# Row maxima of the attention scores: one reduction over two PSUM banks for two query tiles, in place of one reduction per tile

## What is computed

```python
x = x + xattn(ctx, layernorm(x), mask)      # 8 heads of 32, 512 queries x 512 keys per batch and head
scores = einsum('bthd,bshd->bhts', q, k) / sqrt(32)
scores = where(src_mask == 0, -inf, scores)
attn = softmax(scores, axis=-1)             # the row maximum is subtracted before exp
x = x + ffn(layernorm(x))                   # 16 experts, top 8, and one shared expert
```

## Time and profile before

| what | value |
|---|---|
| median of 3 runs | 1065.43 us (1065.13 to 1066.44) |
| profiled execution: span from the first to the last instruction | 1056.2 us |
| median less that span | 9.2 us |
| mean granted TensorE clock | 0.992 |
| busy share of the span | PE 96%, PEld 73%, DVE 61%, ACT 44%, POOL 37% |
| max matmuls | 256, the first at 27.6 us, the last at 426.5 us |
| reductions to maxima | 256, 683 ns median, 173.3 us together |

### The profile page before, as it was taken

How to read it: one execution, slowest core, us unless ns; L and a number is a source line. 1 busy time by engine, 2 the same in 40 slices (tenths; PEclk the granted TensorE clock), 3 DMA queues, 4 the chain that set the end, 5 groups by cost and what they waited for, 6 DMA issues and landing times.

```text
span 1056.2 us, 14941 instructions
## 1 busy us (share of the span) xinstructions
PE 1012.5 (96%) x5198; PEld 773.3 (73%) x5198; DVE 647.5 (61%) x1469; ACT 465.9 (44%) x865; POOL 389.0 (37%) x355
## 2 busy tenths in 40 slices
PE   4789999999999998899999999999999999999998
PEld 3656767676767665567888888888888888888886
DVE  5877777877777557355565555555555555555544
ACT  3346565656665646545323323333333333332322
POOL 3379797879797967345210010010010100100000
PEclk9899999999999999999999999999999999999999
DMA  7343433434333223324222121121220230221220
GB/s 239 104 131 78 131 81 111 108 84 131 73 110 75 65 65 105 92 86 131 75 80 61 52 80 50 61 81 40 72 80 31 71 90 20 91 80 31 93 68 20
DMA packets 65674, 87.87 MB, mean 83 GB/s; under 512 B 10720, under 2 KB 31088, under 8 KB 65600
## 3 DMA queue, kind: packets, MB, share of 16 engines
q1 hardware_dynamic: 63680, 84.83, 28.0%
q10 hardware_dynamic: 1920, 2.10, 0.6%
HBM read 56.97 MB, written 4.46 MB: 58 GB/s over the span
## 4 chain that ended last, share of the span: by engine, by line
PE 91%; DVE 4%; ACT 2%; SPq 1%; issue 1%; DMA 1%; POOL 0%; DVEq 0%; ACTq 0%
PE ps L653 50%; PE pst L653 18%; PE ps L732 6%; PE ps L759 5%; PE pst L748 5%; PE ps L659 4%; PE ps L772 1%; DVE mx L1201 1%; ACT e_buf L868 1%; SPq L606 1%; PE ps L811 1%; SPq L541 1%; ACT ctx_h L868 0%; DVE wsrc_l L1148 0%; PE ps L812 0%
## 5 line engine op out<-in xcount | busy, mean ns | idle before, releaser
L653 PE MATMUL ps<-x_h,weights 128*128 128x512 f32 x1088 | 365.6, 397 | 1.4 <-DVE x L1194 0.8
L653 PEld LDWEIGHTS ps<-x_h,weights 128*128 128x128 f32 x1088 | 204.5, 188 | 51.8 <-issue 1.0
L1201 DVE TENSOR_REDUCE mx<-ps 128x1 f32<-128x512 f32 x256 | 173.3, 685 | 81.8 <-PE ps L732 80.9
L868 ACT ACTIVATE hh<-qb 128x512 fp32r<-128x512 f32 x136 | 86.0, 632 | 296.4 <-DVE qb L1315 273.7
L653 PE MATMUL ps<-x_l,weights 128*128 128x512 f32 x544 | 214.6, 395 | 0.0
L653 PE MATMUL pst<-hh,weights 128*128 128x512 f32 x544 | 194.6, 399 | 0.0
L1304 DVE TENSOR_TENSOR qb<-ps,sg 128x512 f32<-128x512 f32 x136 | 94.1, 692 | 160.2 <-PE ps L653 153.8
L868 ACT ACTIVATE e_buf<-pst 128x512 f32<-128x512 f32 x256 | 147.4, 596 | 92.8 <-PE pst L748 81.8
L1317 DVE TENSOR_TENSOR hl<-qb,hh 128x512 fp32r<-128x512 f32 x136 | 94.3, 693 | 95.0 <-ACT hh L868 95.0
L1407 POOL TENSOR_TENSOR e_sums<-e_sums,e_buf 128x1024 f32<-128x1024 f32 x60 | 143.5, 2391 | 7.2 <-ACT e_buf L868 1.2
L1359 POOL TENSOR_SCALAR ve<-mv 128x4 f32<-128x4 f32 x8 | 1.8, 226 | 347.1 <-DVE mv L1242 347.1
(11 more groups left out here) (159 smaller groups left out, 1391.5 us busy)
## 6 DMA issues: line engine op xcount, KB each, us to landing
cb<-combine_scratch SPq DMA_DIRECT2D x128, 256.0 KB, 3.2
q_stack<-q_h SPq DMA_DIRECT2D x128, 64.0 KB, 2.0
k_stack<-k_h SPq DMA_DIRECT2D x124, 64.0 KB, 2.0
ctx_raw<-in_ctxT SPq DMA_DIRECT2D x7, 1024.0 KB, 5.2
q_stack<-q_l SPq DMA_DIRECT2D x64, 64.0 KB, 2.0
out_x<-ob SPq DMA_DIRECT2D x16, 256.0 KB, 2.2
k_stack<-k_l SPq DMA_DIRECT2D x62, 64.0 KB, 2.0
x<-in_x SPq DMA_DIRECT2D x7, 512.0 KB, 6.5
```

Of the source, the lines that this page charges most:

```text
L653: ins = engine.matmul(dst, lhsT, rhs, start=start and n == 0, stop=stop and n == len(terms) - 1)
L868: return engine.activation(dst, src, func, **kw)
L1201: engine.tensor_reduce(MX[:, g % 2, h // 2, h % 2, q:q + 1], bank(step), AX.X, ALU.max).then_inc(sem("max"), 1)
```

## The change

The max steps are now made for every second query tile only: 128 steps `("max", g, h, q)` with q = 0 or 2, each at the time that the even one had. Both banks are one tensor, `psm`, of shape 128 x 2 x 512. A step issues two matmuls on TensorE, into the one and the other bank, and the semaphore goes up after the second. VectorE reduces both banks in one instruction to two columns of `MX`. Each step owns both banks, so it waits for the reduction of the step just before it. Nothing else in the table of times is changed.

```diff
--- before.py
+++ after.py
@@ -143,7 +143,7 @@
     for h, t in enumerate((-2, -1, 0, 1)):
         at(t, ("stack", 1, h))
 
-    for j in range(16 * NG):
+    for j in range(0, 16 * NG, 2):
         at(j - MAX_LEAD, ("max", j // 16, j // 4 % 4, j % 4))
     for g in range(NG):
         for a in range(2):
@@ -306,9 +306,9 @@
          or s[0] == "attend" and s == sums_step(s[1]) or s[0] == "k" and s[2] == 0 or s[0] == "v" and s[3] == 0 or s in (("gating", 0, 0), ("grows", 0), ("grows", N_GROWS - 1))]
 RING2 = [s for s in ORDER[ORDER.index(("first_ends",)):]
          if s[0] in ("turn_x2", "turn_c", "store") or (s[0] == "gating" and s[2] == 0)]
-BANK = ({s: i % 2 for i, s in enumerate(MAXES)} | {s: 2 + i % 3 for i, s in enumerate(RING3)}
+BANK = ({s: 0 for s in MAXES} | {s: 2 + i % 3 for i, s in enumerate(RING3)}
         | {s: 4 + i % 2 for i, s in enumerate(RING2)})
-BANK_BEFORE = dict(zip(MAXES[2:], MAXES)) | dict(zip(RING3[3:], RING3)) | dict(zip(RING2[2:], RING2))
+BANK_BEFORE = dict(zip(MAXES[1:], MAXES)) | dict(zip(RING3[3:], RING3)) | dict(zip(RING2[2:], RING2))
 
 
 
@@ -346,7 +346,8 @@
                 made[name] = top.enter_context(nc.semaphore(name))
             return made[name]
 
-        P = [top.enter_context(nc.psum_tensor(f"ps{i}", [128, 512], F32)) for i in range(6)]
+        PM = top.enter_context(nc.psum_tensor("psm", [128, 2, 512], F32))
+        P = [PM[:, i, :] for i in range(2)] + [top.enter_context(nc.psum_tensor(f"ps{i}", [128, 512], F32)) for i in range(2, 6)]
         YP = top.enter_context(nc.psum_tensor("pst", [128, 2, 512], F32))
         GP = [[P[2 * pair + a][:, :] for a in range(2)] for pair in PAIR]
         OP = P[5]
@@ -728,12 +729,14 @@
                     z = g % 2
                     pe.wait_ge(*stacked(g, h))
                     pe.wait_ge(*row_loaded(g))
-                    ps = own_bank(step)
-                    engine.matmul(ps, QS[z][0:97, h, 128 * q:128 * q + 128], KS[z][0:97, h, :], start=True,
-                                  stop=True).then_inc(sem("s_max"), 1)
+                    own_bank(step)
+                    for n in range(2):
+                        tok = slice(128 * (q + n), 128 * (q + n) + 128)
+                        ins = engine.matmul(PM[:, n, :], QS[z][0:97, h, tok], KS[z][0:97, h, :], start=True, stop=True)
+                    ins.then_inc(sem("s_max"), 1)
                 elif kind == "shift":
                     _, g, a = step
-                    pe.wait_ge(sem("max"), COUNT["max", g, 2 * a + 1, 3])
+                    pe.wait_ge(sem("max"), COUNT["max", g, 2 * a + 1, 2])
                     ps = own_bank(step)
                     turns([(ps[0:8, 0:128], MX[:, g % 2, a, :, :].rearrange("p h q -> p (h q)"))], sem("mx_t"))
                 elif kind == "scores":
@@ -1198,7 +1201,7 @@
                     dve.wait_ge(sem("s_max"), COUNT[step])
                     if g >= 2:
                         dve.wait_ge(sem("mx_t"), COUNT["shift", g - 2, h // 2])
-                    engine.tensor_reduce(MX[:, g % 2, h // 2, h % 2, q:q + 1], bank(step), AX.X, ALU.max).then_inc(sem("max"), 1)
+                    engine.tensor_reduce(MX[:, g % 2, h // 2, h % 2, q:q + 2], PM[:, :, :], AX.X, ALU.max).then_inc(sem("max"), 1)
                 elif kind == "recip":
                     g = step[1]
                     dve.wait_ge(sem("s_turned"), g + 1)
```

## The result

The changed kernel takes **1075.22 us** (median of 4 runs, 1073.3 to 1075.92), the kernel before 1065.28 us beside it (4 runs, 1063.55 to 1066.44). The medians differ by 9.9 us. The ratio estimated from the single executions is 1.0105, with a 95% interval of 1.0082 to 1.0127: slower by 11.2 us, between 8.7 and 13.5 by the ends of the interval.

The account below looks back on a forecast made before the run. TensorE was taken to bound the attention phase, so its waits for merged reductions lengthen the kernel. 7.8 + 0.4 + 1.0 + 0.2 = 9.4, rounded to +9.5 us on span 1056.2, plus 9.2, gave 1075 us, range 1069 to 1082.

Parts of the forecast that it names:

- Rival 4: Two banks in one reduction cost as much as two reductions, 1.37 us: +2.2, 1077 us; chance 0.07.
- The pair's cycle: First matmul of a pair to the earliest first matmul of the next: 0.23 + 0.43 + 1.22 + 0.05 = 1.93 us.
- Place A: Steady attention batch, pairs at 237.11 and 238.49, 1.38 us apart, with projections behind: stall of 0.55 us.
- Place B: Steady attention batch, first step, 247.26 to 248.44, 1.18 us, ahead of the transposes of `xn`: stall of 0.75 us.
- Second step of B: 248.44 to 249.92, 1.48 us: stall of 0.45 us, hidden in TensorE's wait for an exponential, so it costs nothing.
- The sum over the pattern: Stalls at Place A and Place B, repeated in six attention batches: 6 x (0.55 + 0.75) = 7.8 us.
- The start: 27 to 66 us, where DVE is busy and PE waits for it: +0.2 us, between -2 and +2.
- The last batch: Last attention batch: +0.5 us at 389.29 for a longer reduction, +0.5 at 420.75 to 422.15; together +1.0.
- The 9.2 us between it and the median: Offset from the profiled execution's span to the median, added to the predicted span of 1065.7 for 1075 us.
- Rival 1: DVE's fixed cost comes off the path at the start and in the last batch: 1057 us, at most 1049; chance 0.08.
- Rival 2: Stalls at Place A and Place B eat idle time further on: no change, +-2 us, 1065 us; chance 0.08.
- Rival 3: PE's idle time at Place B drops the clock in the batches: +24.5 us, 1090 us; chance 0.05.

Follow-up runs that it names:

- early_before: The kernel before, with the transposes of the second half of `xt` moved 1.2 steps earlier; 1072.32 us, ratio 1.0087.
- order_only: The changed kernel with its paired matmul order kept, but each bank released and reduced by itself; 1066.63 us, ratio 1.0012.
- the ordinary execution: An execution of an unchanged copy of the kernel before, traced as a second reference; 1066.17 us, span 1063.9.
- spread_a: The changed kernel with only the pair behind place A moved, by 0.3 of a step; 1066.61 us, ratio 1.0034.
- half_cols: The changed kernel with the merged reduction reading only 256 of the 512 columns of each bank; 1065.09 us, ratio 1.0006.
- single_wait: The kernel before, each max matmul made to wait for the reduction just before it, not two steps back; 1175.47 us, ratio 1.1076.

## Why the prediction was right, and where its sizes were off

The forecast was 1075.0 us in a range of 1069 to 1082; the kernel takes 1075.22.

- **The price of a merged reduction**, 1.22 us: 1219 ns. The rule of the Trainium skill in "VectorE: DVE Perf Modes", section "The TRN2 errata", gives 1192 for it; the trace doesn't agree, here as little as for 512 elements. Rival 4 (1.37 us) has fallen.
- **DVE relieved of 19 us**: 15.7. The reductions' own time fell by 17.2 us (173.3 to 156.1), and DVE's other work took 1.5 more. Reductions that stand directly behind each other overlap: the two of 1.28 us in the row of early_before end 1.28 us after the first begins, where two times 0.69 are 1.37. So the pairs that were removed had cost less than their durations. It had no weight in the time, as the step said.
- **The pair's cycle**, 1.93 us: 1.95 at the first stall of B (254.46 to 256.41), but 2.04 at A and 2.14 for the next pair of B (256.41 to 258.55). In these two the matmul begins 0.15 us after the reduction's end, not 0.05, and in the last the pair's own matmuls stand 0.33 apart.
- **Place A**, 0.55: 0.73. The step set the late weight loads behind a stall off against small gaps that would vanish. They didn't vanish; that term was mis-sized by 0.18 per batch. **Place B**, 0.75: 0.76. **Second step of B**, nothing: confirmed, the stall takes the place of the wait for the exponential.
- **Not foreseen**: 0.18 per batch at the start of its second half, which comes with issuing the matmuls in pairs (order_only has it too). And once in the kernel, a gain: in the batch from 150 to 200 us PE had waited 0.95 us for `gate_sb`, since that DVE instruction took 2.14 us:

```profile
195.61 2.14 DVE L1229 TENSOR_SCALAR gate_sb<-gate_sb,gate_r 16x256 f32<-16x256 f32 x1
...
197.80 0.29 PE L659 MATMUL ps<-ident_sb,gate_sb 16*128 16x16 f32 x2 [0.95 <-DVE gate_sb L1229]
```

  In the changed kernel the same instruction, then at 201.09, takes 0.34 us, and nobody waits; this batch gives some 1.3 us back.
- **The sum over the pattern.** Five of the six repetitions lie between scores 36 and 216. The step gives 5 x 1.30 = 6.5 there, and 7.1 was measured: 1.67 a batch, not 1.30, and one batch that gives most of it back. Two errors of opposite sign.
- **The start**, with the first repetition in it (stalls at 91.96 and 102.74, like the others): 1.3 + 0.4 + 0.2 by the steps, +0.5 against the ordinary execution. The bound of 2 us holds, but this is no clean comparison: in that execution the clock was at 0.74 from 60 to 70 us and here at 0.89. The steps looked at DVE alone. PE's longest wait after 60 us is the one for an exponential behind ScalarE's wait for a DMA; it is 4.06 us in that execution, 1.35 in the one of the rows, and 2.26 in the changed kernel.
- **The last batch**, +1.0: +2.9 between scores 216 and 248, with 1.4 given back behind it, where no max step stands: the clock between score 248 and the last one was 0.80 in the ordinary execution, 0.89 in the changed kernel and 1.00 in the trace of the rows, and the stretch takes 17.4, 16.0 and 14.5 us. So these 1.4 us aren't the change's. Here the steps overlooked a place: before, matmuls at 399.22 and 400.40 stand 1.18 us apart, as at B, and in the changed kernel the pair there waits:

```profile
411.62 0.73 PE L735 MATMUL psm<-k_stack,q_stack 97*128 97x512 f32 x2 [0.85 <-DVE mx L1204]
```

  So the term should have been 1.75. The rest I can't split: the clock is below full in this stretch in all three traces (0.91, 0.83, 0.85 from 410 to 430 us), and spread_a shows that moving pairs changes this batch by more than the stalls at A and B.
- **The step that failed is the base.** "The 9.2 us between it and the median" isn't something around the span, but 2.3 us around it and 7 us by which the traced execution was quick. Against that execution the changed kernel's span is 16.8 us longer (1073.0 against 1056.2), and no step of the sum has the other 7 us; against an ordinary one it is 9.1 longer, against a sum of 9.4. The forecast came out because the sum was put on the median, not because the base was understood. And that 9.4 meets 9.1 is in part luck: the mechanism and the stalls of the steady batch are right, but the pattern was 0.6 us too small, the start 1.4 too large, and the last batch with what follows it 0.5 too small (1.0 against 1.5).
- **Rival 1** (faster, 1049 to 1057) fell: DVE's work went down and its share of the chain up. The rule in the Trainium skill, "Perfetto Trace Analysis", section "Optimizing Scalar/DVE Operations", says that grouping can help an engine that is saturated; DVE, at 61%, isn't, and the trace agrees, as does the half_cols run, where 9.7 us less DVE work per batch gained nothing. The rule of the Trainium skill on rotating banks, in "Perfetto Trace Analysis", section "Optimizing Tensor Performance", agrees too, with A and B as its price. **Rival 2** (absorbed) fell but for the second step of B. **Rival 3** (the clock) fell: 1.00 in the steady batches. But it was nearer than its 0.05 says: in early_before, with 1.1 us idle at B, the clock fell in two of six batches, to 0.55 in one stretch of five microseconds, and in single_wait it is 0.95 over a batch.

What stays open: what decides, from one execution to the next, how long the DMA wait at the start is and whether the clock is granted in full behind PE's gaps there, in the last batch and behind it, and why the changed kernel never shows a quick execution like those of before (of 8 runs none was under 1073.3; in its trace both stretches are below full clock, 0.89 at 60 to 70 us and 0.85 at 410 to 430). And the last 2 us per batch of single_wait.

## What to carry to other kernels

Merging two steps that share a rotating pair of buffers saves the fixed cost of an instruction and gives up the rotation. The fixed cost counts only if that engine is waited for; the rotation counts wherever the producer comes back sooner than one matmul pair, one eviction and their latencies take (here 1.95 to 2.14 us). Compare that cycle with the smallest distances between steps, not with their mean (3.1 us here): 2 of 16 distances in a batch made most of the loss, and moving the steps there apart took 1.2 of the batch's 1.6 us away. Moving a step can also open a new wait elsewhere, as early_before shows.

Before a sum is put on a traced span, look whether that execution's own time is the median's. If it isn't, take a second trace of the same kernel: what differs between the two can't be put down to a change.

## What the runs showed of the chip that I had not expected

- A VectorE reduction out of PSUM costs by its elements, whether they lie in one bank or two: 685 ns (512 in one), 687 (512 in two), 953 (768), 1219 (1024); 1.04 ns per element and about 0.15 us besides.
- Executions of the kernel before differ by up to 9 us, while their steady batches agree to 0.03 us (49.43 and 49.46). Between the two traces compared, the difference comes with the clock granted behind long gaps of TensorE (1.00 or 0.50 at 65 to 70 us, 1.00 or 0.71 at 445 to 450) and with a longer wait behind a DMA at the start (PE idle for 1.35 or 4.06 us).
- The same idle time need not have the same effect on the clock: at six waits of 1.11 to 1.16 us in one trace, early_before, it fell twice (to 0.55 in one stretch) and stayed at 1.00 four times.
- Reducing the slack of every max matmul from two steps to one cost 10.8% (1.1076), nearly twice the sum of the shortfalls in a batch; with stalls of 0.66 us on average (82.8 us in 125), TensorE's clock was granted at 0.95 over a batch, against 1.00 before.
